# One low part per step moved from GpSimd to VectorE, and another cut in two, in a one-core gated cross-attention block

## The reference

```
n  = layernorm(x)
Q, K, V = n @ Wq.T, ctx @ Wk.T, ctx @ Wv.T       # 32 query heads, 8 key/value heads of 128
x  = x + tanh(g0) * (softmax(causal(Q K / sqrt(128))) V) @ Wd.T
f  = layernorm(x)
W' = W * (su @ sv)                               # for each of gate, up, down (512 x 1792)
x  = x + tanh(g1) * (silu(f @ gate') * (f @ up')) @ down'
```

## Time and profile before

| what | value |
|---|---|
| median of 3 runs | 1372.1 us (1368.18 to 1373.67) |
| the profiled execution, its own time | 1370.94 us |
| its span, first to last instruction | 1369.1 us |
| busy: PE / DVE / POOL / ACT | 1356.6 / 959.8 / 954.4 / 561.1 us |
| quads, attention, FFN (from the trace) | about 54 to 500, 500 to 950, 950 to 1369 us |
| granted TensorE clock | 1.0 in all slices |

### The profile page before, as it was taken

The page is one execution under the profiler, slowest core; times in us unless marked ns, Lnnn a source line. Parts: engine busy times, 40 slices in busy tenths (PEclk is TensorE's granted clock), DMA queues, the critical chain, the costliest instruction groups (busy, mean ns, idle before and its releaser), DMA issues.

```text
span 1369.1 us, 21420 instructions
## 1 busy us (share of the span) xinstructions
PE 1356.6 (99%) x7770; PEld 1112.6 (81%) x7770; DVE 959.8 (70%) x1465; ACT 561.1 (41%) x950; POOL 954.4 (70%) x883
## 2 busy tenths in 40 slices
PE   8999999999999999999999999999999999999998
PEld 8988788888888878778787877788888888888887
DVE  6388677665565677666667877774789888766776
ACT  5455555555444523232223334232344434334333
POOL 5599989999887946445454666573787787666664
PEclk9999999999999999999999999999999999999999
DMA  8386787777978866454445556621322331311121
GB/s 294 123 264 220 238 265 237 270 250 234 335 256 294 283 232 224 154 165 129 153 162 150 185 154 200 200 65 45 78 56 68 92 85 47 123 54 47 47 69 70
DMA packets 158057, 226.47 MB, mean 165 GB/s; under 512 B 43264, under 2 KB 89600, under 8 KB 155904
## 3 DMA queue, kind: packets, MB, share of 16 engines
q1 hardware_dynamic: 157952, 225.09, 51.0%
HBM read 155.32 MB, written 69.73 MB: 164 GB/s over the span
## 4 chain that ended last, share of the span: by engine, by line
PE 83%; POOL 10%; DVE 2%; issue 2%; ACT 1%; DMA 1%; SPq 0%; DVEq 0%; ACTq 0%; POOLq 0%
PE bank L616 65%; POOL wa_lo L1676 5%; PE bank L888 4%; PE bank L890 4%; PE bank L766 4%; PE bank L889 4%; PE bank L742 3%; POOL ws L1664 1%; POOL ws L1667 1%; POOL ws L1665 1%; POOL ws L1669 1%; DVE xc L1274 1%; PE bank L659 0%; DMA er_raw<-in_sf_r 0%; POOL xb L1645 0%
## 5 line engine op out<-in xcount | busy, mean ns | idle before, releaser
L616 PE MATMUL bank<-xc,wa_hi 128*128 128x512 f32 x896 | 277.7, 391 | 0.8 <-ACT s L1012 0.8
L616 PE MATMUL bank<-wd_hi,o_hi 128*128 128x512 f32 x512 | 202.9, 396 | 0.5 <-issue 0.5
L616 PE MATMUL bank<-wd_lo,o_hi 128*128 128x512 f32 x512 | 199.5, 390 | 0.0
L616 PE MATMUL bank<-wd_hi,o_lo 128*128 128x512 f32 x512 | 199.2, 389 | 0.0
L616 PEld LDWEIGHTS bank<-xc,wa_hi 128*128 128x128 f32 x896 | 167.3, 188 | 38.1 <-ACT s L1012 2.5
L616 PE MATMUL bank<-xc,wa_lo 128*128 128x512 f32 x448 | 174.5, 390 | 0.0
L1063 ACT ACTIVATE o_hi<-bank 128x512 fp32r<-128x512 f32 x128 | 69.5, 595 | 228.3 <-PE bank L766 151.1
L1477 DVE SCALAR_TENSOR_TENSOR X<-bank,tg,X 128x512 f32<-128x512 f32 x221 | 154.4, 741 | 0.0
L616 PE MATMUL bank<-x_hi,wf_hi 128*128 128x512 f32 x392 | 152.6, 389 | 0.1
L616 PE MATMUL bank<-x_hi,wf_lo 128*128 128x512 f32 x392 | 152.5, 389 | 0.0
L616 PE MATMUL bank<-x_lo,wf_hi 128*128 128x512 f32 x364 | 141.6, 389 | 0.0
(11 more groups left out here) (175 smaller groups left out, 3157.0 us busy)
## 6 DMA issues: line engine op xcount, KB each, us to landing
q_scratch<-q_st SPq DMA_DIRECT2D x32, 1024.0 KB, 4.8
q_sb<-q_scratch SPq DMA_DIRECT2D x64, 512.0 KB, 4.8
w_raw<-in_wq SPq DMA_DIRECT2D x32, 512.0 KB, 4.1
wd_raw<-in_wd SPq DMA_DIRECT2D x16, 1024.0 KB, 4.8
f_raw<-ffn_eff_scratch SPq DMA_DIRECT2D x28, 512.0 KB, 3.7
er_raw<-in_sf_r SPq DMA_DIRECT2D x42, 256.0 KB, 4.3
e_raw<-in_wf SPq DMA_DIRECT2D x42, 256.0 KB, 5.4
ffn_eff_scratch<-e_eff SPq DMA_DIRECT2D x42, 256.0 KB, 5.2
```

The source lines that it names most:

```text
L616: last = pe.matmul(to, a, b, start=(start and n == 0), stop=(stop and n == 3 * len(pairs) - 1), skip_group_check=onto)
```

## The change

The first of the three low parts of a left operand (`left_lo`, blocks 0 to 1, 512 elements) is no longer made by POOL but by DVE, in a new function `first_left_lo(w + 1)`, issued in quad q right behind t1. The same for the context slices 2 to 7 (`first_c_lo(q + 1)`, in quads 1 to 6; slices 0 and 1 stay on POOL). Two new semaphores, `v_wa` and `v_cl`, count them; who waited for three parts on POOL's semaphore now waits for two there and for one on DVE's: TensorE at the start of a quad, ACT once, and SP in `load_c` and `load_w`. Before, POOL made the low parts of slice j two quads ahead of their use; now the first of them is made one quad ahead.

`x_lo(m)` becomes two operations: blocks 4 to 6 (768 elements) at the end of quad q in X_SPLIT, behind `lr_lo`, and blocks 0 to 3 (1024 elements) in quad q + 1 behind t1, where the whole stood before. Its semaphore counts to 16 in place of 8.

```diff
--- before.py
+++ after.py
@@ -195,6 +195,7 @@
     v_c1 = sem("v_c1")
     g_t, g_s, g_wa, g_wd, g_xn = sem("g_t"), sem("g_s"), sem("g_wa"), sem("g_wd"), sem("g_xn")
     g_t2, g_fs, g_fw, g_dn, g_c22 = sem("g_t2"), sem("g_fs"), sem("g_fw"), sem("g_dn"), sem("g_c22")
+    v_cl, v_wa = sem("v_cl"), sem("v_wa")
     g_ct, g_cl, a_ch, v_ws, a_wvh, v_wvl = (sem("g_ct"), sem("g_cl"), sem("a_ch"), sem("v_ws"), sem("a_wvh"),
                                             sem("v_wvl"))
     p_k, p_xt, p_e = sem("p_k"), sem("p_xt"), sem("p_e")
@@ -240,6 +241,10 @@
 
         return j + 3 if j else 0
 
+    def c_parts(j):
+
+        return 3 * min(j, 2) + 2 * max(j - 2, 0)
+
     def c_buffer(i):
         return c_raw[i % 2] if i else c_first
 
@@ -362,7 +367,9 @@
                 sp.wait_ge(a_chi, i - 1)
                 sp.wait_ge(c_split, i - 2)
             if i >= 6:
-                sp.wait_ge(g_cl, 3 * (i - 4))
+                sp.wait_ge(g_cl, c_parts(i - 4))
+                if i > 6:
+                    sp.wait_ge(v_cl, i - 6)
             sp.dma_start(c_buffer(i)[:, :, :], ctx_t[LOADS[i]]).then_inc(d_c[i % 2], 16)
 
         def store_k(c):
@@ -390,7 +397,8 @@
 
                 sp.wait_ge(p_p[3], NV)
             else:
-                sp.wait_ge(g_wa, 3 * (w - 1))
+                sp.wait_ge(g_wa, 2 * (w - 1))
+                sp.wait_ge(v_wa, w - 1)
             if w < NK:
                 raw = w1[2 * w:2 * w + 2].rearrange("e p d -> p e d")
             else:
@@ -529,7 +537,7 @@
                 load_X(q - Q0 - NHP - 1)
             if q == Q0 + NHP + 8:
 
-                sp.wait_ge(v_xlo, 8)
+                sp.wait_ge(v_xlo, 16)
                 for n in range(4):
                     sp.wait_ge(d_ko[n], 16 * NCH // 2)
                 sp.wait_ge(d_vo[0], 16 * V_BUFFER.count(0))
@@ -683,13 +691,16 @@
                 pe.wait_ge(a_c11, q)
             if q < NV:
                 pe.wait_ge(a_ch, 3 * (q + 1))
-                pe.wait_ge(g_cl, 3 * (q + 1))
+                pe.wait_ge(g_cl, c_parts(q + 1))
+                if q >= 2:
+                    pe.wait_ge(v_cl, q - 1)
             else:
                 pe.wait_ge(a_wa, 3 * (q - NV + 1))
-                pe.wait_ge(g_wa, 3 * (q - NV + 1))
+                pe.wait_ge(g_wa, 2 * (q - NV + 1))
+                pe.wait_ge(v_wa, q - NV + 1)
             if q >= Q0:
                 pe.wait_ge(a_xhi, 4 * (block_of(q) + 1))
-                pe.wait_ge(v_xlo, 4 * (block_of(q) + 1))
+                pe.wait_ge(v_xlo, 8 * (block_of(q) + 1))
             product(q, 1, 0, 0, 0)
             if q:
                 pe.wait_ge(v_t2, q)
@@ -958,7 +969,7 @@
         def x_columns(m):
             a.wait_ge(p_xt, 2 * m + 1)
             if m:
-                a.wait_ge(v_xlo, m)
+                a.wait_ge(v_xlo, 2 * m)
             a.activation(xb[:, 1:3, :, :], bank[4][:, :].rearrange("p (n k t) -> p n k t", n=2, k=2),
                          ACT.Copy).then_inc(a_xt, 1)
             a.wait_ge(p_xt, 2 * m + 2)
@@ -982,7 +993,8 @@
             a.wait_ge(d_wq[p], 16 * (w // 2 + 1))
             if w == 0:
 
-                a.wait_ge(g_cl, 3 * NCH)
+                a.wait_ge(g_cl, c_parts(NCH))
+                a.wait_ge(v_cl, NCH - 2)
             elif w == 1:
 
                 a.wait_ge(p_p[3], NV)
@@ -1268,10 +1280,24 @@
             v.wait_ge(d_x, 16 * (m + 1))
             ln_bn(lambda p: x_st[:, p, :])
 
-        def x_lo(m):
+        def x_lo(m, part):
             v.wait_ge(a_xhi, m + 1)
-            to = xc[m // 4][:, m % 4]
-            v.tensor_tensor(to[:, 1], xb[:, 1:8, :, :], f32(to[:, 0]), ALU.subtract).then_inc(v_xlo, 1)
+            to, n = xc[m // 4][:, m % 4], slice(0, 4) if part else slice(4, 7)
+            v.tensor_tensor(to[:, 1, n], xb[:, 1 + n.start:1 + n.stop, :, :], f32(to[:, 0, n]),
+                            ALU.subtract).then_inc(v_xlo, 1)
+
+        def first_c_lo(j):
+            to, raw = cc[:, j % 4], by_block(c_buffer(c_load(j))[:, :, :])
+            v.wait_ge(a_ch, 3 * j + 1)
+            v.tensor_tensor(rows_of(to[:, 1, 0:2].rearrange("p n k t -> p (n k) t")), raw[:, :, 0],
+                            rows_of(f32(to[:, 0, 0:2]).rearrange("p n k t -> p (n k) t")),
+                            ALU.subtract).then_inc(v_cl, 1)
+
+        def first_left_lo(w):
+            v.wait_ge(a_wa, 3 * w + 1)
+            v.tensor_tensor(wa_lo[w % 2][:, 0:2, :, :].rearrange("p n k d -> p (n k d)"), w_raw[w_buffer(w)][:, 0, :],
+                            f32(wa_hi[w % 2][:, 0:2, :, :]).rearrange("p n k d -> p (n k d)"),
+                            ALU.subtract).then_inc(v_wa, 1)
 
         def lr_lo(m):
             v.wait_ge(a_lr, 2 * (m + 1))
@@ -1293,6 +1319,10 @@
             v.wait_ge(p_p[6], q + 1)
             v.wait_ge(a_s1, q + 1)
             v.tensor_tensor(t1[:, :], bank[1][:, :], s1[:, :], ALU.add).then_inc(v_t1, 1)
+            if 2 <= q + 1 < NCH:
+                first_c_lo(q + 1)
+            if 0 <= w + 1 < NW:
+                first_left_lo(w + 1)
             if q == 0:
                 lr_lo(0)
             if q in APPLY:
@@ -1300,7 +1330,7 @@
                     stats1(APPLY[q])
                 ln_moments(APPLY[q])
             if q - 1 in X_SPLIT:
-                x_lo(X_SPLIT[q - 1])
+                x_lo(X_SPLIT[q - 1], 1)
             if q == NQ - 2:
                 maxima(0)
             if q == NQ - 1:
@@ -1333,6 +1363,8 @@
                 effective(E_AT[q])
             if q + 1 in E_AT:
                 lr_lo(E_AT[q + 1])
+            if q in X_SPLIT:
+                x_lo(X_SPLIT[q], 0)
             if q in STATS and q in X_SPLIT:
                 stats1(STATS[q])
             if q == NQ - 2:
@@ -1365,7 +1397,7 @@
             v.wait_ge(g_p, 2 * p + 2)
             if p == 2:
 
-                v.wait_ge(g_wa, 3 * NW)
+                v.wait_ge(g_wa, 2 * NW)
             if p >= 4:
                 v.wait_ge(p_o, 2 * p - 2)
             v.transpose(pt_of(p)[:, :, :].rearrange("p n k -> p (n k)"),
@@ -1603,7 +1635,7 @@
             else:
                 g.wait_ge(d_c[c_load(j) % 2], 16 * ((c_load(j) + 1) // 2))
                 g.wait_ge(a_ch, 3 * j)
-                g.wait_ge(g_cl, 3 * j)
+                g.wait_ge(g_cl, c_parts(j))
             b11, b12, b21, b22 = raw[:, :2, 0], raw[:, :2, 1], raw[:, 2:, 0], raw[:, 2:, 1]
             g.tensor_tensor(to[0], b12, b11, ALU.subtract).then_inc(g_ct, 1)
             g.tensor_tensor(to[2], b22, b12, ALU.subtract).then_inc(g_ct, 1)
@@ -1614,10 +1646,11 @@
 
         def c_combinations_lo(j):
             to, raw = cc[:, j % 4], by_block(c_buffer(c_load(j))[:, :, :])
-            g.wait_ge(a_ch, 3 * j + 1)
-            g.tensor_tensor(rows_of(to[:, 1, 0:2].rearrange("p n k t -> p (n k) t")), raw[:, :, 0],
-                            rows_of(f32(to[:, 0, 0:2]).rearrange("p n k t -> p (n k) t")),
-                            ALU.subtract).then_inc(g_cl, 1)
+            if j < 2:
+                g.wait_ge(a_ch, 3 * j + 1)
+                g.tensor_tensor(rows_of(to[:, 1, 0:2].rearrange("p n k t -> p (n k) t")), raw[:, :, 0],
+                                rows_of(f32(to[:, 0, 0:2]).rearrange("p n k t -> p (n k) t")),
+                                ALU.subtract).then_inc(g_cl, 1)
             g.wait_ge(a_ch, 3 * j + 2)
             g.tensor_tensor(rows_of(to[:, 1, 2]), raw[:, 2:, 1], rows_of(f32(to[:, 0, 2])),
                             ALU.subtract).then_inc(g_cl, 1)
@@ -1672,6 +1705,8 @@
             p, raw, sums = w % 2, w_raw[w_buffer(w)], ws[w_buffer(w)]
             raws = (raw[:, 0, :], raw[:, 1, D // 2:], sums[:, :, :, :].rearrange("p n k d -> p (n k d)"))
             for n, (part, raw) in enumerate(zip((slice(0, 2), slice(2, 3), slice(3, 7)), raws)):
+                if n == 0:
+                    continue
                 g.wait_ge(a_wa, 3 * w + n + 1)
                 g.tensor_tensor(wa_lo[p][:, part, :, :].rearrange("p n k d -> p (n k d)"), raw,
                                 f32(wa_hi[p][:, part, :, :]).rearrange("p n k d -> p (n k d)"),
```

## The result

| | before | changed |
|---|---|---|
| median, 16 runs each | 1370.2 us (1368.18 to 1373.67) | 1374.05 us (1372.66 to 1377.58) |
| ratio | | 1.0030, 95% interval 1.0022 to 1.0037 |
| profiled execution, own time / span | 1370.94 / 1369.1 us | 1372.88 / 1371.1 us |
| quads, first matmul of 0 to end of 43 | 443.7 us | 445.1 us |
| TensorE behind the quads, first to last matmul | 867.0 us | 867.0 us |

The account below looks back on a forecast made before the run. TensorE was taken to bound the kernel, its stalls alone winnable. Profiled 1370.9 us, less 2.7 for late stalls, plus 2.6 for early waits, gave 1370.8; working from 1371.5 between profile and runs, it gave 1371.4, range 1366.5 to 1375.5.

Parts of the forecast that it names:

- The bound: TensorE, busy 99% of the span, sets the pace; only its stalls can be won, 6.6 us at most.
- Behind the quads nothing changes: Attention and FFN, after the quads, keep their operations; no change in time was forecast there.
- about 0.5%: How far from no change a measurement of this kernel was said to tell: 6.9 us.
- Step (5): Quads 1 to 4: load_c waits for the moved context operation, load_lr queues behind it; +2.6 us (0 to 6.9).
- step (3): x_lo in two, its first part ahead of the next t1 in DVE's idle time: cost 0, except in quad 4.
- Step (4): POOL's relief removes stalls in quads 13, 21, 25 (-1.6) and at quad 10 (-1.1): -2.7 us together (-3.6 to 0).
- one pattern: Product 2 stalls of quads 13, 21 and 25, 0.54 us each, all laid to POOL's backlog making ACT's s1 late.
- Step (2): DVE gains the moved operations behind t1, 1.4 us each, hidden in 2.7 us of room before product 6: cost 0.
- rival D: Behind t1, DVE becomes what TensorE waits for, t2 too late: 8.4 us price, 1379.8 us, chance 0.09.
- A: The forecast case: late stalls in the quads go, early ones come; 1369 to 1374 us, chance 0.52.
- rival C: Late stalls stay, held by something else than POOL or x_lo long in quad 9; early ones come: 1374.1 us, chance 0.13.
- The prediction's own sign of being wrong: Forecast wrong if the span moves over 5 us either way, or new stalls appear behind quad 12.

Follow-up runs that it names:

- Experiment 4: Changed kernel with load_lr put ahead of load_c on the DMA queue, all else as changed: ratio 1.0020 to the kernel before.
- the second profile: The changed kernel profiled and timed once more, unchanged: ratio 1.0026 to the kernel before; its quads took 447.3 us.
- experiment 7: Kernel before with only the context part moved to VectorE; left operand's part on GpSimd, x_lo whole: ratio 1.0015.
- Experiment 14: Kernel before, nothing moved, with GpSimd's 1024-element operation of the left operand in two of 512: ratio 1.0031.
- experiments 6: Kernel before with only x_lo cut in two; both low parts stay on GpSimd: ratio 1.0009.
- experiment 3: Kernel before with only the left operand's part on VectorE; context part on GpSimd, x_lo whole: ratio 0.9991.
- experiment 2: Changed kernel with x_lo in one operation again, behind t1 of quad q+1; both moved operations on VectorE: ratio 1.0009 to the kernel before.

## Why the prediction was wrong

**The bound** was right: TensorE's pace, its 867 us behind the quads untouched, and all of it a matter of few stalls under 0.5%. "Behind the quads nothing changes" missed the 0.6 us at the end of the span. And a measurement of this kernel tells more than "about 0.5%": the interval of the result is 1.0022 to 1.0037.

**Step (5), the queue behind load_c,** held in place and size: +2.6 us forecast, 2.8 and 2.0 in two profiles. load_c and load_lr went out 1.9 us later (2.3 forecast, though the prediction's own terms, 71.6 - 68.98, give 2.6), the transposes of quad 2 stood 0.5 us (1.0), and the lap through quads 3 to 6 cost 2.2 (1.6). Experiment 4 shows that it is the queue in quads 2 and 5. Quad 4, which gives 0.8 of the 2.0 us in the second profile, is another matter: it stays at 11.4 us with the queue in order and goes to 10.13 with x_lo whole, so it belongs to step (3), and the sum of (5) is partly luck.

**Step (4), the gain,** came in size (13, 21 and 25: 2.0 us, forecast 1.6; the start of quad 10 and quad 30: 0.8, forecast 1.1 for quad 10, in the first profile; 0.3 lost in the second, by quad 30). Its cause was told too simply, for the three stalls are not "one pattern". In quads 21 and 25 the wait does go through GpSimd, by its shift that stands for er (experiment 7). Experiment 14 fits that: 0.2 us more on GpSimd brings such a shift to all four quads. In the changed kernel shift starts 0.5 us into quad 21 in place of 2.15. But experiments 6 and 7 lose the stalls of these two quads with nothing taken from GpSimd there, since 0.3 to 0.6 us bring shift ahead of er. Relief is enough for them; it isn't needed. In quad 13 the kernel before waited for a load, not for GpSimd, and that 0.7 us of the gain came by another way than the prediction's: er_raw landed 2.2 us into the quad before and 0.3 after. Why it landed earlier is not shown.

**Step (3) failed:** "The first part lies ahead of the next t1, where DVE idled 1.17 us for ACT's s1. Cost 0, except in quad 4." I priced that part at 0.9 us, its work, and gave the price of a stand for GpSimd to the moved operations only, though both read two SBUF inputs. It takes 1.98 us on average (1.78 in the second profile) and 3.04 in quad 19. The room there was 1.17 us of idle time and 1.57 from t1's end to product 7, 2.7 in all, less than the 3.04. The stand was also of the change's own making: by taking 1.4 us from the head of GpSimd's work in each quad it brings GpSimd's longest operation from 5.2 us into quad 19 (252.22, the quad begins at 247.0) to 2.7 (251.81, the quad begins at 249.1), ahead of t1, where VectorE has er, el and the new part to do. In quads 11 and 27 er stands for it and the part's 1.38 us come on top; experiment 6 shows the same part nearly free while the long operation stays late. I had counted GpSimd's relief as gain alone. So most of what was gained at product 2 in quads 13, 21 and 25 (2.0 us) was given back at product 7 in 11, 19 and 27 (1.6), and the sum of terms, which had a gain of 2.7 against a loss of 2.6, lacked a third term. It measures 0.21% with both operations moved (2.9 us: 1.0030 against 1.0009), 0.32% with the left part alone, and is not told from 0 where neither is moved.

**Step (2)** took 1.4 us for a moved operation: 1.64 and 1.08 were measured, 1.84 in experiment 3, still without a stall of product 6 behind t2. The room was measured to the wrong consumer, though: c12 is begun 1.9 us behind t2 and product 5 comes 1.36 us behind product 6, so c12 is late first, as product 5 of quad 16 (experiment 2) and quad 20 (experiment 3) shows. The rival D had put the slow mechanism, VectorE as what TensorE waits for, behind t1, at t2. It came ahead of t1, where I had not looked for it, and at half the price. The rule that the prediction weighed (the Trainium skill, "SBUF — State Buffer", "Who interferes with whom": the engine that starts first holds the shared ports for its whole instruction) fits every collision shown; the fault was to apply it to one of two new operations.

**The chances** gave 0.91 to a change within 0.5%, and that was so. The likeliest case was A, with late gains and early losses, which is what the two traces show; its own range, 1369 to 1374, was short by the missing term. That 1374.05 lies in the wide range and beside the number of rival C (1374.1) is luck: C wanted the late stalls to stay, and they went. The prediction's own sign of being wrong, new stalls behind quad 12, came true in quads 19 and 27, and in 15 in the second profile.

What stays open: which order of two starts an execution falls into was seen, not controlled; what makes a load of er_raw land 2 us late in quads 13 and 30, and the 0.6 us at the end, were not followed up; nor was why the cut costs nothing beside the context part (1.0015 without, 1.0008 with it, not told apart).

## What to carry to other kernels

Price every operation that is added to VectorE with two SBUF inputs as its work plus a stand for the longest GpSimd operation beside it, and put it where the next consumer has that much room. Ask of an engine that is relieved what it will now do earlier, and what it meets there: here its longest operation moved onto VectorE's busiest stretch. When a buffer's last reader moves to a later point, look at what is queued behind the refill on the DMA queue: here one swap of two loads made 0.2% (1.0009 to 0.9987 with x_lo whole). Try the parts of a combined change one by one; here one part alone was no slower than before (0.9991) and the whole was slower (1.0030). Follow stalls that look alike one by one to what released them: of three here, two went through GpSimd and one through a load.
